# Windowed attention: the position bias of every head group added by TensorE, one plain minimum a group on VectorE, and the copies ahead of the small ones on ScalarE and VectorE

## The reference, cut to what matters

```
q, k, v = split(x @ qkv_weight.T + qkv_bias)          # per head: 128 x 8
attn = (q * 8 ** -0.5) @ k.T + bias[h]                # 128 x 128 for each window and head; bias[h] from bias_table
attn = softmax(attn, axis=-1)
out  = (attn @ v) @ proj_weight.T + proj_bias
h    = h + out
```

## Time and profile before

| | us |
|---|---|
| median of 3 runs | 1490.92 (1488.49 to 1492.17) |
| the profiled execution | 1492.72 |
| its span, first to last instruction | 1490.8 |
| TensorE busy in the span | 1335.4 |
| stage 2, from the first scores to the last scores | 237.1 to 593.6 |
| one loop iteration of stage 2 in steady state | 22.43 |

### The profile page before, as it was taken

How to read it: one execution, slowest core, us unless ns; L and a number is a source line. 1 busy time by engine, 2 the same in 40 slices (tenths; PEclk the granted TensorE clock), 3 DMA queues, 4 the chain that set the end, 5 groups by cost and what they waited for, 6 DMA issues and landing times.

```text
span 1490.8 us, 43422 instructions
## 1 busy us (share of the span) xinstructions
PE 1335.4 (90%) x15780; PEld 880.4 (59%) x15780; DVE 887.4 (60%) x2815; ACT 860.3 (58%) x2649; POOL 613.7 (41%) x967
## 2 busy tenths in 40 slices
PE   6998997888888888799999998799999999969998
PEld 2446874444444444577777777456666666446665
DVE  3775774555555555577878886234555555655664
ACT  3975663777777777455555555235555555635553
POOL 5000113555655655435555564412333333225554
PEclk9997996999999999899999999659999999969999
DMA  8300000000000000000000000000000000000001
GB/s 222 70 1 0 1 1 1 2 0 0 0 0 0 0 0 0 2 3 0 0 0 0 0 0 1 1 0 2 0 0 0 0 0 1 0 0 10 15 14 23
DMA packets 10094, 13.79 MB, mean 9 GB/s; under 512 B 9136, under 2 KB 9136, under 8 KB 9520
## 3 DMA queue, kind: packets, MB, share of 16 engines
q1 hardware_dynamic: 10032, 12.95, 3.5%
HBM read 10.85 MB, written 2.10 MB: 9 GB/s over the span
## 4 chain that ended last, share of the span: by engine, by line
PE 72%; ACT 10%; DVE 9%; issue 6%; POOL 1%; DMA 1%; ACTq 0%; DVEq 0%; POOLq 0%; SPq 0%
PE bank L1318 6%; PE bank L588 5%; PE bank L591 5%; PE bank L632 5%; PE bank L1655 4%; PE bank L145 4%; PE bank L1673 4%; PE bank L1312 4%; ACT big L689 3%; PE bank L1007 2%; PE bank L1277 2%; PE bank L1342 2%; ACT big L696 2%; PE bank L1034 2%; PE bank L324 2%
## 5 line engine op out<-in xcount | busy, mean ns | idle before, releaser
L527 POOL TENSOR_TENSOR big<-big 128x512 f32<-128x512 f32 x128 | 133.0, 1039 | 153.7 <-DVE big L725 153.6
L632 PE MATMUL bank<-cst,big 128*128 128x128 f32 x512 | 80.1, 279 | 53.5 <-ACT big L696 53.0
L632 PEld LDWEIGHTS bank<-cst,big 128*128 128x128 f32 x512 | 59.7, 142 | 104.5 <-issue 86.4
L1390 POOL TENSOR_TENSOR big<-g_a,g_b 64x64 f32 x128 | 40.0, 312 | 191.1 <-DVE g_a L1380 191.1
L929 POOL TENSOR_TENSOR big<-big 128x512 f32<-128x512 f32 x64 | 65.6, 1045 | 113.8 <-DVE big L1183 113.8
L689 ACT ACTIVATE big<-big 128x128 f32<-128x128 f32 x256 | 100.0, 405 | 1.2 <-DVE big L737 1.2
L1709 ACT ACTIVATE big<-bank 128x512 f32<-128x512 f32 x128 | 66.2, 603 | 50.4 <-PE bank L1655 50.4
L1576 POOL TENSOR_TENSOR big<-big 128x512 f32<-128x512 f32 x48 | 60.9, 1270 | 74.8 <-DVE big L1779 72.2
L1357 ACT ACTIVATE g_r<-bank,g_bias 128x64 f32<-128x64 f32 x128 | 40.2, 314 | 88.6 <-PE bank L1318 88.5
L689 ACT ACTIVATE big<-bank,big 128x128 f32<-128x128 f32 x256 | 90.5, 370 | 0.0
L1342 PE MATMUL bank<-cst 128*128 128x256 f32 (+1 forms) x256 | 88.3, 426 | 0.0
(11 more groups left out here) (271 smaller groups left out, 3661.1 us busy)
## 6 DMA issues: line engine op xcount, KB each, us to landing
big<-x_dram SPq DMA_DIRECT2D x12, 512.0 KB, 8.0
cst<-consts_dram SPq DMA_DIRECT2D x1, 3364.5 KB, 22.4
out_dram<-h SPq DMA_DIRECT2D x8, 256.0 KB, 2.6
cst<-consts_dram SPq DMA_DIRECT2D x3, 256.0 KB
cst<-consts_dram SPq DMA_DIRECT2D x1, 279.5 KB, 3.0
a_proj_padded<-consts_dram SPq DMA_DIRECT2D x8, 2.0 KB
cst<-consts_dram SPq DMA_DIRECT2D x8, 2.0 KB
cst<-consts_dram SPq DMA_DIRECT2D x2, 4.0 KB
```

Source lines behind the costliest of these rows:

```text
L527: nc.gpsimd.tensor_tensor(P, P, a_rs[t % 4].unsqueeze(2).to_broadcast([128, 4, 128]), ALU.mult).then_inc(a_n_r, 1)
L632: m = nc.tensor.transpose(bank(4)[:, 128 * k:128 * (k + 1)], a_P[tb % 4][:, 128 * k:128 * (k + 1)], eye)
```

## The change

TensorE adds the bias for every group. `bias(t)` is split off from `scores(t)`: the bias of the even group t+1 follows the two scores matmuls in the odd slot, and the bias of an odd group t+1 is issued in the even slot t, behind the transposes and `attended`. VectorE takes one `tensor_reduce` for every group, ScalarE's exponential reads PSUM for every group, and the even bank is free only after the exponential and no longer after the minimum. In ScalarE's slot the small copies `rows` and `queries` move behind the exponential and the copy of bank 4. In VectorE's slot the copy of bank 4 moves ahead of `keys` and of the addition to h.

```diff
@@ stage2_pe, scores
             if t >= 4 or exists(i, -1):
-                if t % 2:
-                    pe.wait_ge(a_e_r, i * 8 + (t - 3))
-                else:
-                    pe.wait_ge(a_mx_r, i * 8 + (t - 3))
+                pe.wait_ge(a_e_r, i * 8 + (t - 3))
             r = slice(32 * u, 32 * u + 32)
-            m = nc.tensor.matmul(scores_bank(t), a_q[l][r, :], a_kz[l][r, :], start=True, stop=not t % 2)
-            if t % 2:
-                m = nc.tensor.matmul(scores_bank(t), eye, c("a_bias", 512, 1024), start=False, stop=True)
-            m.then_inc(a_sc_r, 1)
+            nc.tensor.matmul(scores_bank(t), a_q[l][r, :], a_kz[l][r, :], start=True, stop=False)
+
+        def bias(t):
+            half = 512 * (t % 2)
+            nc.tensor.matmul(scores_bank(t), eye, c("a_bias", half, half + 512), start=False, stop=True).then_inc(a_sc_r, 1)
@@ stage2_pe, slot
                 for d in (1, 2):
                     if exists(i, (t + d) // 8):
                         scores(i + (t + d) // 8, (t + d) % 8)
+                if exists(i, (t + 1) // 8):
+                    bias(t + 1)
+            if t % 2 == 0 and exists(i, 0):
+                bias(t + 1)
             if u == 0:
@@ stage2_act, slot
-            if u == 0 and exists(i, l, N2 - 1):
-                rows(i + l, 1 - l)
...
-                if tb % 2 and (tb >= 4 or exists(ib, -1)):
+                if tb >= 4 or exists(ib, -1):
...
-                    raw = scores_bank(tb)[:, 128 * k:128 * (k + 1)] if tb % 2 else P
+                    raw = scores_bank(tb)[:, 128 * k:128 * (k + 1)]
...
-            if u == 1 and exists(i, l, N2 - 1):
-                queries(i + l, 1 - l)
             ib, tb = back(i, t, 3)
             if tb % 2 and exists(ib, 0):
                 act.wait_ge(a_pt_r, ib * 8 + (tb + 1))
                 nc.scalar.copy(a_PT[tb % 4], bank(4)).then_inc(a_pta_r, 1)
+            if u == 0 and exists(i, l, N2 - 1):
+                rows(i + l, 1 - l)
+            if u == 1 and exists(i, l, N2 - 1):
+                queries(i + l, 1 - l)
@@ stage2_dve, slot
-                if t % 2 == 0 and (t >= 4 or exists(i, -1)):
-                    v.wait_ge(a_pt_r, i * 8 + (t - 3))
-
-                if t % 2:
-                    m = nc.vector.tensor_reduce(a_mx[t % 4], scores_bank(t).rearrange("p (j k) -> p j k", j=4), X, ALU.min)
-                else:
-                    nc.vector.memset(spare[:, 24 + t:25 + t], 0.0)
-                for k in range(0 if t % 2 else 4):
-                    m = nc.vector.tensor_tensor_reduce(a_P[t % 4][:, 128 * k:128 * (k + 1)], scores_bank(t)[:, 128 * k:128 * (k + 1)],
...
+                m = nc.vector.tensor_reduce(a_mx[t % 4], scores_bank(t).rearrange("p (j k) -> p j k", j=4), X, ALU.min)
                 m.then_inc(a_mx_r, 1)
+            ib, tb = back(i, t, 3)
+            if tb % 2 == 0 and exists(ib, 0):
+                ...
+                nc.vector.tensor_copy(a_PT[tb % 4], bank(4)).then_inc(a_ptd_r, 1)
             if u == 1 and exists(i, l, N2 - 1):
                 keys(i + l, 1 - l)
```

More of the change, by code:

```diff
@@ L658, in stage2_pe @@
         scores(0, 1)
+        bias(0)
         pipelined(pe, slot)
@@ L728, in slot @@
                 v.wait_ge(a_sc_r, i * 8 + (t + 1))
-                if t % 2 == 0 and (t >= 4 or exists(i, -1)):
-                    v.wait_ge(a_pt_r, i * 8 + (t - 3))
-                if t % 2:
-                    m = nc.vector.tensor_reduce(a_mx[t % 4], scores_bank(t).rearrange("p (j k) -> p j k", j=4), X, ALU.min)
-                else:
-                    nc.vector.memset(spare[:, 24 + t:25 + t], 0.0)
-                for k in range(0 if t % 2 else 4):
-                    m = nc.vector.tensor_tensor_reduce(a_P[t % 4][:, 128 * k:128 * (k + 1)], scores_bank(t)[:, 128 * k:128 * (k + 1)],
-                                                       c("a_bias", 512 * (u % 2) + 128 * k, 512 * (u % 2) + 128 * (k + 1)), 1.0, 3e38,
-                                                       ALU.add, ALU.min, a_mx[t % 4][:, k:k + 1])
-                m.then_inc(a_mx_r, 1)
+                m = nc.vector.tensor_reduce(a_mx[t % 4], scores_bank(t).rearrange("p (j k) -> p j k", j=4), X, ALU.min)
+                m.then_inc(a_mx_r, 1)
+            ib, tb = back(i, t, 3)
+            if tb % 2 == 0 and exists(ib, 0):
+                v.wait_ge(a_pt_r, ib * 8 + (tb + 1))
+                if tb >= 4 or exists(ib, -1):
+                    v.wait_ge(a_av_r, ib * 8 + (tb - 3))
+                nc.vector.tensor_copy(a_PT[tb % 4], bank(4)).then_inc(a_ptd_r, 1)
             if u == 1 and exists(i, l, N2 - 1):
@@ L746, in slot @@
                 nc.vector.tensor_tensor(hp, hp, bank(3)[:, 128:256].rearrange("p (b c) -> p b c", c=C), ALU.add).then_inc(a_h_r, 1)
[L747 to L752, removed]
             if isinstance(i, int) and i == N2 and t in (2, 4):
```

## The result

| | before | changed |
|---|---|---|
| median of 5 runs | 1490.92 us (1487.66 to 1492.17) | 1501.11 us (1500.03 to 1504.19) |
| ratio, 95% interval | | 1.0076 (1.0057 to 1.0094) |
| span of the profiled execution | 1490.8 us | 1499.9 us |
| a half iteration of stage 2, mean of 28 | 11.21 us | 11.75 us |

The changed kernel is 0.8% slower, 10 us. I had forecast slower, by 1.4%, 21 us, with a range of 1500 to 1521: the sign is right, and the time stands at the very foot of the range.

The account below looks back on a forecast made before the run. TensorE's own work plus two holes bound each 11.21 us half; +0.64 (biases +1.94, new hole +0.57, old holes and tails out) over 29 halves gave +18.5, start +1.2, end +1.2: 1490.92 + 20.9 = 1511.8 us, range 1500 to 1521.

Parts of the forecast that it names:

- the old holes and their tails: Stage 2, ahead of transposes in u = 1 and u = 3: 1.73 us a half given back, plus tails of 2 x 0.07.
- two biases a half: Stage 2, TensorE: 64 added bias matmuls, two a half at 0.97 us each, adding 1.94 us a half.
- the new hole: Ahead of the scores of u = 3: TensorE waits for `spread`, 0.50 to 0.57 us once a half.
- My term of 0.97: TensorE's price of one added bias in us, start to next start, with bounds of 0.86 and 1.05.
- The start: Stage 2 from 237.07 to 265.53: five more biases and two new holes, less old holes and a clock dip; +1.2 us.
- the second spell at 1.2 GHz: Clock dip at 258 us in the start: goes if TensorE no longer idles, worth about 3 us.
- The end: Last half of stage 2, 590.60 to 598.13: two biases against idle time of 1.02; +1.2 us (0.9 to 1.9).
- my likeliest case: Whole kernel: old holes close, biases added, new hole opens; 1511.8 us, 1.4% slower, 70% chance.
- A, the hole doesn't show: Rival, scores of u = 3: no new hole appears there; +4.4 us, 1495.3 us; 12%.
- B, ScalarE late: Rival, transposes of u = 3 wait for ScalarE's copy of bank 4: 14.5 us more, 1526 us; 11%.
- C, a bias that overlaps: Rival, TensorE: the added bias overlaps its neighbours at 0.53 us, so the kernel is faster, 1485 us; 4%.
- the estimate in the prediction: TensorE: 131 ns spacing and four FP32 passes give 0.52 us a bias, 1.05 a half, fitting into the holes.

Follow-up runs that it names:

- experiment 5: Experiment 4's kernel with the odd bias moved into the even slot and a lower count for `spread`, even bias still on VectorE: 1427.35 us, 0.9582 of before.
- experiment 1: The changed kernel with a lower count for `spread`, leaving out the four groups of the lane at work: 1482.43 us, 0.9951 of before.
- experiment 4: The kernel before with only the new order of copies on ScalarE and VectorE: 1440.73 us, 0.9677 of before.
- 6: Experiment 4's kernel with the odd bias moved into the even slot and `spread`'s count as it was: 1449.11 us, 0.9713 of before.
- experiment 3: The changed kernel with ScalarE's and VectorE's copies back in the old order: 1543.82 us, 1.0355 of before.
- 7: The changed kernel with both biases in the odd slot behind the scores, and the old count: 1495.18 us, 1.0028 of before.

## Why the prediction was right in sign and half wrong in size

The mechanism held in its main parts. The two old holes close, two biases a half are added, and a new hole opens ahead of the scores because `spread` waits for a count that now comes a slot later. The runs take these apart, in us for a half of stage 2:

| part | predicted | measured | from |
|---|---|---|---|
| the old holes and their tails | -1.87 | -1.94 | before 11.21, experiment 5 9.27 |
| two biases a half | +1.94 | +1.80 | experiment 5 9.27, experiment 1 11.07 |
| the new hole | +0.57 | +0.68 | experiment 1 11.07, changed 11.75 |
| sum | +0.64 | +0.54 | 11.21 to 11.75 is 0.53 from the windows |

In whole runs the same: the order of copies gave 50 us (experiment 4), the moved bias with the old count took 8 (4 to 6), and 64 biases took 52 (6 to changed). The 64 biases alone are experiment 1 against 5: 55.1 us, 0.86 each. The two also differ in VectorE's operations, but TensorE has no idle time in the loop of either, so VectorE holds up nothing there.

My term of 0.97 was over for two reasons. Of the four biases of a half the one in slot u = 0 costs 0.86 to 0.87 and only the other three 0.97; less the two of before at 0.97 each, that makes 1.84. And the transposes take 0.53 from start to start behind a bias, where they take 0.58 behind scores (349.44 to 350.02 in experiment 5), which explains the rest. What stands ahead of a bias goes with its price throughout the loops of these traces: 0.96 to 0.97 behind scores (32 rows) or `attended` (32 columns), 0.85 to 0.87 behind transposes or another bias, which take 128 rows and columns, whatever comes next; why, no run shows. The new hole was right at 0.57 with its tail, and its price was under by the 0.11 that the pair of scores loses behind a hole.

Elsewhere two terms of the sum were mis-sized and one piece was left out, and together they are more than the loop's 3 us.

- *The start*, "I take +1.2, with -1 and +4 as ends": it got 2.2 us shorter, 26.28 against 28.46, outside my ends. The mean granted clock in it is 0.87 where the earlier trace rows has 0.69. The windows of the changed kernel at 243 and 255 us:

```profile
243.00:246.00 3.00, 3.00 (x13) 1.64 (x14) 0.50 (x3) 2.91 (x17) 1.04 (x1) 0.95 0.01 3
...
255.00:258.00 3.00, 3.00 (x20) 1.53 (x19) 0.78 (x2) 2.21 (x12) 0.65 (x1) 1.00 0.00 0
```

  and of the kernel before:

```profile
243.00:246.00 3.00, 3.00 (x7) 1.08 (x7) 1.02 (x8) 1.98 (x11) 1.04 (x1) 0.50 0.00 0
...
255.00:258.00 3.00, 3.00 (x10) 1.51 (x9) 1.03 (x3) 1.78 (x11) 0.54 (x1) 0.50 0.00 0
```

  The clock is at 2.4 GHz from about 243 us on, where before it was at 1.2 until about 247.8, and the second spell at 1.2 GHz, from about 254.6 to 261.4, is gone. I had counted on the second and not on the first. The earlier rise goes with the change: in the four kernels in which TensorE adds every bias (the changed one and experiments 1, 3 and 7) it comes at 242 to 243.5 us, in the six others at 245.6 to 254. That is one trace of each kernel, and what sets the moment stays open. Nor is the clock all of it. In experiment 5 it rose last,

```profile
252.00:255.00 3.00, 3.00 (x24) 1.28 (x23) 1.09 (x2) 1.77 (x9) 0.40 (x1) 0.64 0.00 0
```

  and its start still took only 25.2 us, without added biases. With them, the old order of copies makes the start 28.5 us at a clock of 0.88 (experiment 3), the new one 26.28 at 0.87: so 2.2 us of it are the order's.
- *The end*, "+1.2": the last half and what follows it, up to the last `project`, took +0.45 and -0.19. I had counted two added biases in the last half, and there is one: it has one bias before (593.57) and two after (606.21 and 608.06). The 64 are 5 in the start, 58 in the 29 halves and 1 here; my terms add up to 65. The one that came took the place of a hole of 0.41 ahead of transposes.
- *Behind stage 2* I had counted nothing. The profiled execution of the kernel before takes 883.7 us from the last matmul of its last `project` (607.1) to its end, that of the changed kernel 879.9 (from 620.0). The code there is the same. In the eight experiments this piece takes 878.5 to 883.2, so it differs by 5 us over the ten traces, and the profile of before was the longest. For a sum against one profile, that is an error of a few us whatever the working.

With the spans: -0.5 ahead of stage 2, -2.2 in the start, +14.9 in the 14 iterations, +0.5 in the half after them, +0.5 in the last half, -0.2 up to the last `project`, -3.8 behind it; before rounding they add up to the 9.1 by which the spans differ.

That the time lies inside the range is partly luck. The bounds of my likeliest case were 1504 to 1520, and the foot at 1500 was there for a hole half as large. The hole cost more than I forecast, not less; the biases, the start and the end brought the time down there.

The rivals. *A, the hole doesn't show*, is what experiment 1 made: 1482 and not the 1495 that I had worked out for it, since my half without the hole (11.28) was 0.21 too long. *B, ScalarE late*, did not happen: no transposes wait in the loop. *C, a bias that overlaps*, is out, at 0.97 and 0.87 from start to start. The sustained spacing that the Trainium skill gives in TensorE: Matmul & The Clock Gate, section Back-to-back issue gap, would by the estimate in the prediction make a float32 bias 0.52, and no bias of these traces comes near it: the lowest is 0.85.

The largest miss is none of the sum's terms. I put down the 1.73 us of holes as what the change gives back, and didn't ask how much of that needed the bias at all. Experiments 4 and 5 say none of it. The order of copies alone closes the large hole and takes 50 us off the kernel before; the place of the odd bias, with the lower count, closes the small one. Against experiment 4 the bias part of the change costs 60 us, 4%: 8 for the odd bias's new place under the old count, and 52 for the added biases. The best of these kernels is experiment 5, at 1427.35 us, 4.2% under before.

## What to carry to other kernels

Take a change apart by which piece closes a wait and which piece adds work, and price each alone: here one piece was worth -50 us and the other +60, and the sum hid both. When an instruction that raises a counted semaphore moves, look up everyone who waits for that count, and whether the count asks for more than the buffer needs; the `spread` wait was four groups too strict, free while the bias stood early and 19 us once it stood late. Where the bound engine waits for a ring (transpose, copy, transpose), putting more of its own work in the hole helps only if the ring doesn't pass through something queued behind that work.

## What the runs showed of the hardware that I had not expected

A 512-column float32 matmul with a full weight tile costs 0.97 us from start to start behind a matmul of 32 rows or 32 columns and 0.86 or 0.87 behind one of 128 by 128, as in a stream (0.86). A pair of 32-row, 512-column matmuls in different rows of the array costs 1.06 us when TensorE comes to it without a stop and, but for two cases (1.05 and 1.06), 1.15 to 1.19 when it has waited for GpSimd. A start that is late by 0.07 us goes with the same price: in the earlier trace rows the pair at 374.94 starts 0.42 behind `attended` instead of 0.35, and takes 1.16. The exponentials that read PSUM went from 370 to 374 ns when all of them did so, and the gain over SBUF (406) stayed. The part of the program behind stage 2, the same in all ten kernels, took between 878.5 and 883.7 us.
